# Half of a shared expert moved into the expert tiles, and an output gate moved into the next program

## What is computed

```python
# layer 0, feed-forward: 8 experts of width 176, 2 per token, and a shared expert of width 352
shared = silu(x @ shared_gate_w.T) * (x @ shared_up_w.T) @ shared_down_w.T
out = routed_experts(x) + sigmoid(x @ shared_expert_gate_w.T) * shared
# layer 1, state space layer, behind the convolution y (after gelu)
z = einsum('oh,bhl->bol', glu_W, y) + glu_b          # 2 x 128 rows
y = a * sigmoid(g)                                    # a, g: the halves of z
x = x + ga * (y.T @ out_W.T + out_b + h)              # h: the layer's normed input
# layer 1, feed-forward: 8 experts of width 352, 2 per token
h = layernorm(x) * (1 + cb) + sb
```

## Time and profile before

| | us |
|---|---|
| median of 3 executions (1174.6 to 1175.93) | 1175.41 |
| span of the profiled execution, the only time of its own that is recorded | 1294.9 |
| PE, DVE, ACT, POOL busy in it | 968.1, 843.4, 680.8, 442.2 |
| mean granted TensorE clock | 0.854 |
| first layer's feed-forward block | about 540 to 853 |
| state space core, gate block | about 853 to 953, 953 to 986 |
| second layer's feed-forward block | 986 to 1295 |

### The profile page before, as it was taken

How to read it: one execution, slowest core, us unless ns; L and a number is a source line. 1 busy time by engine, 2 the same in 40 slices (tenths; PEclk the granted TensorE clock), 3 DMA queues, 4 the chain that set the end, 5 groups by cost and what they waited for, 6 DMA issues and landing times. The chain is left out here.

```text
span 1294.9 us, 26945 instructions
## 1 busy us (share of the span) xinstructions
PE 968.1 (75%) x9019; PEld 636.3 (49%) x9019; DVE 843.4 (65%) x2115; ACT 680.8 (53%) x1445; POOL 442.2 (34%) x510
## 2 busy tenths in 40 slices
PE   4656999999999999667576788718665427789990
PEld 2333333443343334344354677617543426679990
DVE  6897899999999996655431645556838555324444
ACT  3773678788788777324423555527022124436660
POOL 5626122332222122143234556510000733564440
PEclk9785799999999999867778989959687557989995
DMA  7235021111111000111110232276533311122216
GB/s 203 74 126 198 3 82 43 35 55 46 35 55 38 26 2 2 40 50 36 35 42 33 63 83 75 69 223 179 140 103 88 98 57 36 59 77 67 64 57 200
DMA packets 116285, 97.16 MB, mean 75 GB/s; under 512 B 15437, under 2 KB 102568, under 8 KB 116152
## 3 DMA queue, kind: packets, MB, share of 16 engines
q1 hardware_dynamic: 101912, 75.29, 20.4%
q0 software_dynamic: 8704, 17.97, 4.1%
q10 hardware_dynamic: 5536, 2.18, 0.6%
HBM read 60.18 MB, written 34.95 MB: 73 GB/s over the span
## 5 line engine op out<-in xcount | busy, mean ns | idle before, releaser
L568 DVE TENSOR_REDUCE part<-sps 128x2 f32<-128x1024 f32 (+2 forms) x307 | 327.6, 1115 | 27.0 <-PE sps L556 15.6
L911 ACT ACTIVATE prob<-tpa 128x1024 f32<-128x1024 f32 (+1 forms) x208 | 193.1, 928 | 45.1 <-PE tpa L857 43.3
L1632 POOL DMA_INDIRECT yk<-yo,place x144 | 146.6, 1018 | 158.1 <-ACT yo L1661 139.6
L743 POOL TENSOR_SCALAR_AFFINE_SELECT prob<-prob 128x512 f32<-128x512 f32 x128 | 80.5, 641 | 310.3 <-ACT prob L911 310.3
L1232 POOL DMA_INDIRECT xg<-h,slot x128 | 126.9, 991 | 152.1 <-DVE slot L1359 96.7
L877 PE MATMUL ops<-prob,vs 128*32 128x512 f32 (+3 forms) x1536 | 157.9, 498 | 0.1
L911 ACT ACTIVATE prob<-tpb 128x512 f32<-128x512 f32 (+1 forms) x224 | 127.2, 568 | 37.3 <-PE tpb L857 37.2
L549 PE MATMUL sps<-qk 48*128 48x512 bf16 (+2 forms) x734 | 132.9, 339 | 11.3 <-DVE part L568 7.6
L1687 DVE COPY place<-xt 128x1 uint32<-128x1 uint32 x144 | 22.1, 153 | 169.5 <-ACT esg L1655 92.5
L1748 PE MATMUL banks<-xT,y 128*128 128x128 f32 x864 | 113.8, 283 | 20.1 <-ACT y L1646 12.2
L1748 PEld LDWEIGHTS banks<-xT,y 128*128 128x128 f32 x864 | 106.5, 198 | 23.6 <-ACT xT L1641 19.3
(11 more groups left out here) (347 smaller groups left out, 1864.8 us busy)
## 6 DMA issues: line engine op xcount, KB each, us to landing
xt<-xg SPq DMA_DIRECT2D x144, 65.0 KB
qk<-term SPq DMA_DIRECT2D x24, 256.0 KB, 2.6
qk<-qk SPq DMA_DIRECT2D x64, 96.0 KB
arena<-kpad SPq DMA_DIRECT2D x6, 1024.0 KB, 12.3
powers<-powr SPq DMA_DIRECT2D x8, 516.0 KB, 5.3
powr<-powers SPq DMA_DIRECT2D x4, 1032.0 KB, 9.3
qk<-qk SPq DMA_DIRECT2D x64, 64.0 KB
h<-yk SPq DMA_DIRECT2D x16, 256.0 KB, 4.9
```

Of the source, the lines that this page charges most:

```text
L568: return nc.vector.tensor_reduce(to, src, AX.X, ALU.max, negate=True)
L743: nc.gpsimd.affine_select(out=blk, in_=blk, pattern=[[0, HQ], [1, P]], compare_op=ALU.is_ge, fill=0.0, base=0, channel_multiplier=-1).then ...
L911: nc.scalar.activation(prob[:, at:at + len(units), 0:n], slot_of(t, m)[:, :, 0:n], ACT.Exp, scale=float(HD) ** -0.5).then_inc(exp_done, 1)
L1632: nc.gpsimd.indirect_dma_start(out=d.yk, out_offset=bass.IndirectOffsetOnAxis(ap=place[:, u:u + 1], axis=0), in_=yo[u][:], in_offset=None) ...
```

## The change

What it does:

- Layer 0: of the 24 chunks of the shared expert only the first 12 (`EARLY`) stay in the routing. In loop step b TensorE does the weights 2b and 2b+1, chunk 3b, the next batch's transposes and logits, chunks 3b+1 and 3b+2, its ranks. Chunks 12 to 23 are done in rounds 0 to 11 of the expert tiles, one a round, behind the round's own work on TensorE, ScalarE and VectorE. They use one pair of banks (turn 1), and the expert tiles one transpose bank less. The ranks' banks move next to the logits'. The experts' tensor stream waits for the first twelve products and four halves only.
- The gating and adding of the shared expert run from tile 24, every 4 tiles.
- Layer 1: `s4_gate` as a block is gone. `gate_parts` gives its steps to the routing's streams. y is loaded by eight DMAs ahead of the weights, six into space that the convolution has left and two into new buffers. The output gate is multiplied into `outT` (`outG`) and into the kept input's scale and shift beforehand, and the kept input is added to x in `s4_core` (`into_x`), so that `residual` is one addition. The shift and scale of the norm move from VectorE to ScalarE (`norm`), in layer 1 alone.
- The streams of layer 1 interleave gate steps with batch 0's and batch 1's routing; the weights' transposes, which use the gate's banks, wait for all eight additions.

The diff, cut:

```diff
+SUMS_AT = 24
-    WEIGHTS_AT = [([2 * b], [2 * b + 1]) for b in range(NB)]
+    WEIGHTS_AT = [([2 * b, 2 * b + 1], []) for b in range(NB)]
     if layer == 1:
         WEIGHTS_AT = [([0, 1], [2]), ([3, 4], [5]), ([6], [7]), ([], [])]
+    EARLY = M * NB
-    rank_ps, total_ps = pT[:, 0:TPB * NE], pT[:, TPB * NE:TPB * NE + NE]
+    rank_ps, total_ps = pl[:, P:P + TPB * NE], pl[:, P + TPB * NE:P + TPB * NE + NE]
-        turn_of_chunk = lambda n: 2 + n + n // M
-        turn_of_weights = lambda e: 2 + (M + 1) * e + M
+        bank_of_half = lambda s: s % 2 if s < NB else 0
+        TURNS = 2 + M
+        turn_of_weights = lambda e: TURNS * (e // 2) + e % 2
+        turn_of_chunk = lambda n: TURNS * (n // M) + 2 + n % M if n < EARLY else 1
...
+        else:
+            for s in range(2 * NB):
+                gate.load(sp, s)
         for e in range(NE):
             load_weights(sp, e)
...
+        def normed_rows(b):
+            for u in range(2):
+                dve.wait_ge(norm_done, 2 * b + u + 1)
+                h = w.h[0][:, b * TPB + 4 * u:b * TPB + 4 * u + 4, 0:C]
+                link(v.tensor_tensor(h, h, w.modr[:, 2 * layer + 1, b:b + 1, :]..., ALU.mult))
+                v.tensor_tensor(h, h, w.modr[:, 2 * layer, b:b + 1, :]..., ALU.add).then_inc(h_done, 1)
...
+        else:
+            gate.gated(dve, 0)
+            gate.gated(dve, 1)
+            gate.residual(dve, 0)
+            gate.gated(dve, 2)
+            gate.residual(dve, 1)
+            statistics(0)
+            gate.gated(dve, 3)
+            shifts(0)
+            gate.residual(dve, 2)
+            normed_rows(0)
+            gate.gated(dve, 4)
+            gate.residual(dve, 3)
+            experts_of(0)
+            gate.gated(dve, 5)
+            gate.residual(dve, 4)
+            places(0)
+            statistics(1)
+            gate.gated(dve, 6)
+            gate.residual(dve, 5)
+            gate.gated(dve, 7)
+            shifts(1)
+            gate.residual(dve, 6)
+            gate.residual(dve, 7)
+            normed_rows(1)
...
+        if layer == 1:
+            for s in range(4):
+                gate.sigmoid(act, s)
         root(0)
+        if layer == 1:
+            norm(0)
+            gate.sigmoid(act, 4)
         batch(0)
...
+                if layer == 1 and b == 0:
+                    for s in range(5, 2 * NB):
+                        gate.sigmoid(act, s)
                 root(b + 1)
+                if layer == 1:
+                    norm(b + 1)
...
+        if layer == 1:
+            gate.gates(pe, 0)
+            for s in range(4):
+                gate.gates(pe, s + 1)
+                gate.project(pe, s)
         batch(0)
...
+            gate.gates(pe, 5)
+            gate.project(pe, 4)
         ranks(0)
+        if layer == 1:
+            gate.gates(pe, 6)
+            gate.project(pe, 5)
+            gate.gates(pe, 7)
+            gate.project(pe, 6)
+            gate.project(pe, 7)
+            pe.wait_ge(gate.x_done, 2 * NB)
         for b in range(NB):
             for e in WEIGHTS_AT[b][0]:
                 transpose_weights(pe, e)
+            if layer == 0:
+                shared_up(pe, M * b)
             if b + 1 < NB:
                 batch(b + 1)
+            if layer == 0:
+                for n in range(M * b + 1, M * b + M):
+                    shared_up(pe, n)
+                    shared_down(pe, n - 1)
+                shared_down(pe, M * b + M - 1)
                 if b + 1 < NB:
                     ranks(b + 1)
...
+    def late_tensor(pe, k):
+        if k <= NU - EARLY:
+            if k < NU - EARLY:
+                shared_up(pe, EARLY + k)
+            if k > 0:
+                shared_down(pe, EARLY + k - 1)
+    def late_scalar(act, k):
+        if k < NU - EARLY:
+            shared_silu(act, EARLY + k)
+        if k >= M + 1 and k % M == 1 and k <= NU - EARLY + 1:
+            shared_out(act, (EARLY + k) // M - 1)
+    def late_vector(dve, k):
+        if k < NU - EARLY:
+            shared_product(dve, EARLY + k)
...
-            if layer == 0 and 8 <= n and n % 8 == 0:
+            if layer == 0 and n >= 0:
+                routed.late_vector(dve, n)
+            if layer == 0 and SUMS_AT <= n < SUMS_AT + 4 * 2 * NB and n % 4 == 0:
...
+                for s in range(NI // 2):
+                    into_x(s)
                 for s in range(NI // 2, 2 * NB):
                     residual(s)
+                    ins = into_x(s)
...
+    def residual(dve, s):
+        dve.wait_ge(o_ps, s + 1)
+        xs = w.x[:, 4 * s:4 * s + 4, :]
+        nc.vector.tensor_tensor(xs, po[:, s % 2, :]..., xs, ALU.add).then_inc(x_done, 1)
```

More of the change, by code:

```diff
@@ L1102, in weights_parts, with route_parts @@
     return load, transposes, copies, clear, w_tr, w_out
-def route_parts(nc, w, d, layer, ctx, bank):
+def route_parts(nc, w, d, layer, ctx, bank, gate):
     NR = NE + 1 if layer == 0 else NE
@@ L1394, in vector_part, with shared_silu, shared_out @@
             if layer == 0:
-                for s in WEIGHTS_AT[b][1]:
-                    products(s)
+                for n in range(M * b + 1, M * b + M):
+                    shared_product(dve, n)
             if b + 1 < NB:
+                if layer == 1 and b + 2 < NB:
+                    shifts(b + 2)
                 places(b + 1)
                 if b + 2 < NB:
-                    rows(b + 2)
+                    (rows, normed_rows)[layer](b + 2)
+    def shared_silu(act, n):
+        cw = cols[n % M]
+        act.wait_ge(g_ps, n + 1)
+        after(act, hid_done, n - 1)
+        nc.scalar.activation(sg[n % 2][0:cw, :], pg[0:cw, turn_of_chunk(n) % 2, 0, :], ACT.Silu).then_inc(s_done, 1)
+    def shared_out(act, s):
+        act.wait_ge(d_ps, M * (s + 1))
+        for j in range(4):
+            t = 4 * s + j
+            ins = nc.scalar.activation(w.sh[:, t, :], pd[:, bank_of_half(s), j * C:(j + 1) * C], ACT.Copy, scale=w.shw[:, t:t + 1])
+        ins.then_inc(sh_out, 1)
     def scalar_part(act):
@@ L1405, in root, with norm @@
             nc.scalar.activation(w.t1[:, tiles_of(b)], w.t1[:, tiles_of(b)], ACT.Sqrt).then_inc(root_done, 1)
+        def norm(b):
+            act.wait_ge(shifted, b + 1)
+            for t in range(b * TPB, (b + 1) * TPB):
+                ins = nc.scalar.activation(w.h[0][:, t, 0:C], w.x[:, t, :], ACT.Identity, bias=shift[:, t:t + 1], scale=w.rstd[:, t:t + 1])
+                if t % 4 == 3:
+                    ins.then_inc(norm_done, 1)
         def transposed(s):
@@ L1422, in exponentials @@
             nc.scalar.activation(w.shw[:, s], lg[:, s, NE], ACT.Exp, scale=-1.0).then_inc(ex_done, 1)
[L1424 to L1438, removed]
-            ins.then_inc(sh_out, 1)
         def batch(b):
@@ L1721, in vector_part @@
                 next(table)
[L1722 to L1724 removed]
+            if layer == 0 and n >= 0:
+                routed.late_vector(dve, n)
+            if layer == 0 and SUMS_AT <= n < SUMS_AT + 4 * 2 * NB and n % 4 == 0:
+                if n == SUMS_AT:
                     dve.wait_ge(routed.sh_out, 2 * NB)
[L1726 removed]
+                (gated, added)[(n - SUMS_AT) // 4 % 2]((n - SUMS_AT) // 8)
     def tensor_part(pe):
@@ L1732, in t_in @@
             pe.wait_ge(x_in[n % UN], 16 * (n // UN + 1))
-            after(pe, in_T, n - 1)
+            after(pe, in_T, n if layer == 0 else n - 1)
             nc.tensor.transpose(pT[n % 2], xt[n % UN][:, 0:C], w.ident[:]).then_inc(in_ps, 1)
@@ L1776, in tensor_part @@
                 down(n - 1)
+            if layer == 0 and n >= 0:
+                routed.late_tensor(pe, n)
     made = Work()
```

266 lines of the change are left out of this document (129 added, 137 removed).

## The result

The changed kernel takes 1167.4 us (median of 18 runs), the kernel before 1174.2 beside it (18 runs): ratio 0.9943, 95% interval 0.9929 to 0.9957, so 6.7 us faster. Forecast were 1159.0, a gain of 16.4, with the range 1144 to 1180. The sign and the range hold. The size does not: less than half of the gain came.

What follows compares the result with a forecast made beforehand. The prediction took order to bound the first routing, GpSimd's 1.265 us a tile to pace layer 0's tiles and VectorE to bound the gate. Layer 0's -4.4 and the gate's -12 took 1175.4 to 1159, range 1144 to 1180.

Steps and rivals of the forecast that it cites:

- The routing saves 25.6: Layer 0's routing: three steps fall from 31.1 to 22 us each, less 1.8 once for batch 3's table of tiles.
- The tiles lose 21.2: Layer 0 behind the last batch's first scatter: 114.2 us to the end of the tiles becomes 135.4.
- the 3.83 a tile: Layer 0, tiles 0 to 11: TensorE's 1.22 us a tile plus 2.61 for a late chunk.
- I cost that wait at nothing: Late tiles of layer 0: the next tile's copy and product behind the late Silu and product, hidden by TensorE's 2.3 us.
- late tiles over 5 us: Layer 0's tiles with a late chunk: a listed sign that the prediction is wrong; 3.8 us each was expected.
- the net of part A: Layer 0 as a whole: 25.6 us saved in the routing, 21.2 lost in the tiles, net -4.4.
- Rival 3: Layer 0's late chunks run serially on one pair of banks: 5.5 us a tile, total +9, 1184 us; chance 0.18.
- The gate, -12: Layer 1's output gate moved into the routing: first scatter 15 us earlier, 5 given back by batch 1, net -12.
- VectorE is the bound: Gate before layer 1's first scatter: VectorE needs 22.5 us for it plus some 19 of routing work, of 47.1.
- 5 given back and 2 gained: Layer 1's routing: batch 1's later slots cost 5 us; rows moved to ScalarE gain 1 us for each of two batches.
- Cold TensorE, rival 2: Layer 0's routing idles TensorE into its low clock: steps of 27 us, total +1, 1176 us; chance 0.12.
- Sums and tables: Layer 0's eight moved sums cost nothing, +10 at most if crowded; ScalarE's two extra table loads lie within waits.

Runs made afterwards that it cites:

- part A alone: Only the layer 0 change (twelve chunks late, sums from tile 24), layer 1 as in the kernel before: ratio 1.0026, 3.1 us slower.
- experiment 1: The kernel before, unchanged, profiled a second time: span 1174.0 us.
- experiment 4: The changed kernel with ScalarE emptying the finished half's bank ahead of the round's late Silu instead of behind it: ratio 0.9884 to the kernel before.
- sixteen (6): Kernel of experiment 4 with sixteen chunks in the routing, eight late, one between transposes, ranks ahead of the last chunk, banks reassigned: ratio 0.9799, 1151.0 us.
- part B alone: Only the gate change in layer 1, layer 0 as in the kernel before: ratio 0.9904, 11.3 us faster.
- experiment 12: Kernel of part B alone, without interleaving: all eight gate steps ahead of batch 0's statistics on every engine: ratio 0.9992 to the kernel before.
- experiment 7: Order and banks of sixteen (6), but with twelve chunks in the routing and twelve late: ratio 0.9905 to the kernel before.
- experiment 9: Kernel of experiment 4 with the eight sums from tile 16, seven tiles apart: ratio 0.9888 to the kernel before.
- experiment 5: Kernel of experiment 4 with the next batch's ranks in layer 0's routing behind the second chunk instead of the third: ratio 0.9879 to the kernel before.

## Why the prediction was right in one part and wrong in the other

All marks are from the first scatter of layer 0, from the traces of single executions; two kernels with the same layer 0 (the changed one and part A alone) differ by 3 us at the last result, so read them to that.

| | scatter, batch 3 | first result | twelve tiles on | last result |
|---|---|---|---|---|
| before (experiment 1) | 85.0 | 106.2 | 126.1 | 217.0 |
| changed | 62.4 | 82.7 | 130.3 | 221.5 |
| part A alone | 62.8 | 83.1 | 127.7 | 218.3 |
| bank emptied first (4) | 62.2 | 82.5 | 120.9 | 212.8 |
| sixteen (6) | 62.2 | 82.5 | 110.7 | 199.6 |

**The routing saves 25.6.** It saves 22.2 to 22.6 (85.0 less 62.8 or 62.4). The new step is 20.8, better than my 22 and near GpSimd's own 20.2; the old one was 28.3 and not 31.1. I took only the "remote" waits, 25.8 us, out of the disturbed execution, and not the rest of its excess, 34.2 us in these steps. (The sum for a step has a slip: 4 x 0.35 + 2 x 0.69, twice, is 5.6 without its links and not 5.2. It decides nothing, since GpSimd sets the step.)

**The tiles lose 21.2.** This is the step that failed. From batch 3's first scatter to the last result it was 131.9 before and is 159.1, or 155.5 with part A alone: 23.5 to 27.1 lost. The 17.4 to the first result was hidden by GpSimd's 20.3, the 3.83 a tile was right, and one wait was left out: "I cost that wait at nothing" covered the Silu and VectorE's product, but ScalarE's four activations per half, 1.14 us together, were in no step, nor was their bank. From batch 3's first scatter to the twelfth result, 59.5 us were forecast; it is 65.8 in the changed kernel and 56.6 with the bank emptied first. The term was a wait of 6.9 us (experiment 4), costed at zero. Of the prediction's own signs of being wrong this is the one that came: late tiles over 5 us, three of twelve.

With only that order changed (4), the stretch is 150.6: 18.7 lost, the net of part A 18.7 - 22.9 = -4.2, where -4.4 was forecast. The medians say about the same: part A's +3.1 less the 6.9 of experiment 4 is -3.8. That this meets the forecast so closely is luck in part: the routing saves 2.7 us less than was said and the tiles lose 2.5 less.

A larger error cancels too. The prediction had 114.2 us from batch 3's first scatter to the last result before, and 135.4 after; they are 131.9 and 155.5 to 159.1. It took GpSimd's 1.265 a tile for the pace wherever no late chunk stands, and everything above it for stalls of the one execution. The undisturbed trace has 1.56 a tile (experiment 1), and the changed kernel is as slow behind its late tiles: from the twelfth result to the last it is 93.3 us, 92.2 before. Only because both kernels have it does the difference not show it.

Rival 3 came nearest to it: it had ScalarE's order as the cause and 5.5 us a tile, but in every late tile instead of every third, and it had the Silu hold the next tile's copy, where it is the emptying of a bank that holds a down product.

**The gate, -12.** Measured -11.3, and the whole's first scatter comes 32.3 us behind the gate's first products (897.17 to 929.50), 32 forecast. With part B alone it comes 158.9 - 143.6 = 15.3 earlier, counted from layer 0's last result; 15 forecast. But two of the reasons fall. "VectorE is the bound" was half of it: TensorE was as full, and experiment 12 shows that the change without its interleaving gains nothing that can be told (medians 1174.5 and 1173.1, 0.9976 to 1.0008), though its first scatter comes 158.9 - 154.5 = 4.4 us earlier. What gains is that TensorE's last gate products and the later operations stand behind batch 0, the other 10.9 us. And batch 1 gives nothing back through its slots: they stand 18.8 us behind batch 0's in part B alone (forecast 21; 14.8 before), still under GpSimd's 16 scatters, whose steps are 20.9 and 20.6 (21.2 and 20.2 before). What is given back is 1.4 us by the last result (206.0 before, 207.4 with part B alone, from layer 1's first scatter) and 0.8 from there to the end (29.9, 30.7), where the forecast had 5 given back and 2 gained. By these marks part B should be worth 13, the runs say 11.3 (9.2 to 13.5); the number held better than its parts.

**Cold TensorE, rival 2.** The clock was lower, as this rival has it: 0.81, 0.83 and 0.75 over the three steps where it was 0.85, 0.88 and 0.94 before, and the logits of every batch take 3.42, the duration of the low level. The rows: a batch's logits in experiment 1; logits and the slots of batch 3 in the changed kernel; logits in experiment 7:

```profile
632.74 1.90 PE L1484 MATMUL banks<-rt,v 128*128 128x9 f32 x16
609.14 3.42 PE L1576 MATMUL banks<-rt,v 128*128 128x9 f32 x16
623.80 0.20 DVE L1393 CAST slot<-slf 128x16 uint32<-128x16 f32 x1
611.13 1.95 PE L1584 MATMUL banks<-rt,v 128*128 128x9 f32 x16
```

It decided nothing, but only just. The slots of batches 1 to 3 are ready 1.6, 1.6 and 1.1 us before their scatters in the changed kernel (624.00 to 625.06 for the last), and 0.8 is the least there is, when GpSimd waits for them (experiment 1). So 0.3 to 0.8 us a step were to spare; in experiment 7 the slots are 7.6 to 9.1 us ahead. The Trainium skill, "TensorE: Matmul & The Clock Gate", Part 1, says that an array that has not been busy runs at half rate; both durations stand in these rows. Whether that rule is what parts them is not shown: in the third step TensorE was busy for 16.9 of 20.6 us at 0.75, and before for 22.1 of 27.6 us at 0.94. By that rule the prediction would have been 1176, and it is experiment 7 that shows why not: 3.42 became 1.95 without any gain.

**Sums and tables.** Both were put at nothing. Experiment 9 shows it for moving the sums. No run tests ScalarE's two additional table loads.

## What to carry to other kernels

When work is moved beside other work, list every instruction that touches its buffers, emptying included, and ask for each how long the buffer's next writer waits and what stands ahead of the emptying on its engine; a single-buffered bank costs almost nothing if it is emptied while the other engine fills something else (4.08 us a round against 3.83). Work may be put into a stage up to the point at which its engine falls behind the one that paces the stage: here four chunks a batch were best among three, four and five. And before operations are taken off the busiest engine, look whether a second engine is as full, for then only another order helps. When both kernels are costed with the same pace, a wrong pace does not show in their difference: compare the forecast of each stage with the trace, and not the net alone.

## What was not expected of the hardware

A profiled execution can be 10% longer than every timed run (1294.9 against 1170 to 1180), with waits of ScalarE for "remote" in the first routing; a second profile of the same kernel took 1174.0 and had none there. The 120 us lay in the first routing (34.2), layer 0's tiles (32.6) and the second layer from its first scatter to its last result (53.4).

A VectorE addition over 128x1024 elements holds back GpSimd's indirect DMA beside it. In the changed kernel's timeline:

```profile
720.23 1.21 DVE L1808 TENSOR_TENSOR x<-x,y 128x1024 f32<-128x1024 f32 x1
720.67 1.87 POOL L1735 DMA_INDIRECT yk<-yo,place  x1 [4.14 <-ACT yo L1764]
722.84 1.07 POOL L1735 DMA_INDIRECT yk<-yo,place  x1 [0.30 <-issue]
```

1.87 us instead of 0.96, so eight sums cost up to 8 x 0.9 = 7 us of the stage in which GpSimd mostly sets the pace. The long scatters move with the sums: they are every eighth in the kernel before, every fourth in the changed one, every seventh in experiment 9, 1.5 to 2.1 us each. The kernel before has seven such scatters, the others eight, so the change hardly felt it.

TensorE's granted clock in the routing differed between kernels whose steps are equally long, 20.2 to 21.7 us. With four chunks a batch it was 1.00, 1.00 and 0.92 over the three steps. With three it was 0.81, 0.83 and 0.75 in the changed kernel, 0.84, 0.92 and 0.83 in experiment 7, but 0.74, 1.00 and 0.92 in experiment 5. So neither the number of chunks nor the order of experiment 7 decides it alone; what does stays open. None of these levels moved the steps.
